# Casting and averaging of the weights moved from ahead of a recurrent scan into its first group

## What is computed

```python
u = x @ W_in + b_in
g = sigmoid(x @ W_gate + b_gate)
h_t = tanh(h_prev @ A + u_t @ Bm)            # 16384 steps, state of 256
y_t = h_t @ C.T + u_t @ D.T
y_t = g_t * y_t + (1.0 - g_t) * x_t
x1 = layernorm(x + (ys @ W_out + b_out + x))
bw = mean(abs(w), axis=1) * sign(w)          # for w1 (4096 x 1024) and w2 (1024 x 4096)
out = layernorm(x1 + gelu(x1 @ bw1.T + b1) @ bw2.T + b2)
```

## Time and profile before

| what | value |
|---|---|
| median of 3 runs | 12,396.43 us (12,390.03 to 12,402.32) |
| the profiled execution: its own time | 12,394.35 us |
| its span on the slowest core, core 4 | 12,392.8 us |
| spans of the eight cores | 12,332.2 to 12,392.8 us |
| PE, matmuls busy | 6,916.0 us (56%) |
| ScalarE busy | 3,273.7 us (26%) |
| VectorE busy | 1,103.9 us (9%) |
| mean granted TensorE clock on core 4 | 0.535 of full speed |
| first tanh of the scan | 734.59 us from the start |

### The profile page before, as it was taken

How to read it: one execution, slowest core, us unless ns; L and a number is a source line. 1 busy time by engine, 2 the same in 40 slices (tenths; PEclk the granted TensorE clock), 3 DMA queues, 4 the chain that set the end, 5 groups by cost and what they waited for, 6 DMA issues and landing times.

```text
span 12392.8 us, 230075 instructions; the slowest of 8 cores (12332.2 to 12392.8 us)
## 1 busy us (share of the span) xinstructions
PE 6916.0 (56%) x92416; PEld 4470.9 (36%) x92416; DVE 1103.9 (9%) x1916; ACT 3273.7 (26%) x17002; POOL 401.8 (3%) x529
## 2 busy tenths in 40 slices
PE   0034445764467545774467544775467645774444
PEld 0023333443335333443335333443335433443323
DVE  0110000210020100210020100200011100210021
ACT  1112222222223222322223222322223222222210
POOL 1000000000000000000000000000000000000000
PEclk9855555555555555555555555555555555555566
DMA  4430001230023101230013201230013200230024
GB/s 120 137 83 1 1 1 31 87 97 1 1 46 121 48 1 26 74 100 17 1 38 110 67 1 21 59 120 17 1 38 98 79 1 14 76 107 6 1 59 131
DMA packets 360872, 631.19 MB, mean 51 GB/s; under 512 B 18272, under 2 KB 191840, under 8 KB 357760
## 3 DMA queue, kind: packets, MB, share of 16 engines
q0 software_dynamic: 110464, 280.89, 8.8%
q1 hardware_dynamic: 249344, 335.58, 8.6%
HBM read 618.23 MB, written 46.14 MB: 54 GB/s over the span
## 4 chain that ended last, share of the span: by engine, by line
PE 45%; DMA 18%; ACT 17%; issue 13%; DVE 5%; ACTq 2%; DVEq 0%; POOLq 0%; POOL 0%; SPq 0%
PE pss L912 18%; ACT h_ring L922 16%; PE psd L192 16%; DMA BW<-bw2d 8%; PE pss L916 4%; PE pss L914 3%; PE pss L915 3%; DMA XSL<-xT 3%; DMA BW<-bw1d 2%; DMA F32P<-w 2%; ACTq L921 1%; DMA bw2d<-RBF 1%; PE pst L192 1%; DMA bw1d<-RBF 1%; ACT H2BF L576 1%
## 5 line engine op out<-in xcount | busy, mean ns | idle before, releaser
L922 ACT ACTIVATE h_ring<-pss 128x2 bf16<-128x2 f32 x16384 | 2921.7, 178 | 8004.1 <-PE pss L916 8003.9
L912 PE MATMUL pss<-h_ring,A_bf 128*128 128x1 bf16 x16383 | 3037.5, 185 | 3355.3 <-ACT h_ring L922 3338.2
L912 PEld LDWEIGHTS pss<-h_ring,A_bf 128*128 128x128 bf16 x16383 | 1764.8, 108 | 5411.2 <-ACT h_ring L922 4954.3
L899 PE MATMUL pss<-ub_ring,I_bf 128*128 128x2 bf16 x16384 | 2965.8, 181 | 1.3 <-DVE ub_ring L463 1.3
L914 PE MATMUL pss<-h_ring,A_bf 128*128 128x1 bf16 x16383 | 2732.3, 167 | 0.0
L915 PE MATMUL pss<-h_ring,A_bf 128*128 128x1 bf16 x16383 | 2711.5, 166 | 0.0
L916 PE MATMUL pss<-h_ring,A_bf 128*128 128x1 bf16 x16383 | 2702.8, 165 | 0.0
L899 PEld LDWEIGHTS pss<-ub_ring,I_bf 128*128 128x128 bf16 x16384 | 1865.8, 114 | 222.1 <-DVE ub_ring L463 1.8
L914 PEld LDWEIGHTS pss<-h_ring,A_bf 128*128 128x128 bf16 x16383 | 1913.2, 117 | 0.0
L915 PEld LDWEIGHTS pss<-h_ring,A_bf 128*128 128x128 bf16 x16383 | 1740.2, 106 | 0.0
L916 PEld LDWEIGHTS pss<-h_ring,A_bf 128*128 128x128 bf16 x16383 | 1710.9, 104 | 0.0
(11 more groups left out here) (91 smaller groups left out, 2148.2 us busy)
## 6 DMA issues: line engine op xcount, KB each, us to landing
BW<-bw2d SPq DMA_DIRECT2D x256, 512.0 KB, 4.4
BW<-bw2d POOLq DMA_DIRECT2D x256, 512.0 KB, 3.9
BW<-bw1d POOLq DMA_DIRECT2D x128, 512.0 KB, 4.8
BW<-bw1d SPq DMA_DIRECT2D x128, 512.0 KB, 4.0
XSL<-xT POOLq DMA_DIRECT2D x32, 1024.0 KB, 11.4
F32P<-w1T SPq DMA_DIRECT2D x8, 2048.0 KB, 9.8
F32P<-w2T SPq DMA_DIRECT2D x32, 512.0 KB, 3.9
F32P<-w SPq DMA_DIRECT2D x32, 512.0 KB, 3.5
```

What stands on the lines that cost most here:

```text
L899: m0 = eng.matmul(p[:, :], I_bf[:], ub_ring[:, :, slot * G + tl: slot * G + tl + 1], start=True, stop=False)
L912: m1 = eng.matmul(p[:, 0:1], A_bf[:, 0, 0:128], rhs0, start=False, stop=False)
L922: sc_.activation(h_ring[:, :, slot * G + tl: slot * G + tl + 1], p[:, :], AFT.Tanh).then_inc(semh["SS"], 1)
```

## The change

The change moves two pieces of the boot into the planning of group 0, behind plan_uub(1). g_wcast now counts on a semaphore of its own, WCQ, and each of its 16 pairs first waits for the scan to have come to step 256 + 24 x pair, at most G - 64. The 40 loads and sums of absolute values (plan_alpha_consts) wait, load by load, for step 28 x k, k = 0 to 39. The scaling of a1n and a2h is a VectorE item of its own behind the sums, and the item of the boot keeps half_col and bgh8 alone, waiting only for the start loads. Each gelu gets one more wait, for that scaling. The load of F32P0 for group 0 waits for WCQ in place of GXQ. The sign passes stay where they were.

```diff
--- before.py
+++ after.py
@@ -110,7 +110,7 @@
            nc.alloc_psum_tensor("pst1", [128, W], F32)]
 
     sem_names = ["LDW", "TS", "SS", "GX", "GXQ", "GHX", "SYQ", "OUT",
-                 "VDS", "SDS", "PEB2", "GB2"]
+                 "VDS", "SDS", "PEB2", "GB2", "WCQ"]
     sem_names += [f"MMS{i}" for i in range(6)]
     semh = {}
     semc = {n: 0 for n in sem_names}
@@ -264,23 +264,24 @@
 
     def g_wcast(g):
         c = 0
+        pj = 0
         for (srcm, dstm) in ((Wg, wg_d), (Wo, wo_d)):
             for k in range(DC):
                 bounce = H2BF[:, 0:D // H, :] if H <= D else H2BF[:, 0:1, 0:D]
+                g.wait_ge(semh["SS"], min(256 + 24 * pj, G - 64))
+                pj += 1
                 if c > 0:
-                    g.wait_ge(semh["GXQ"], c)
+                    g.wait_ge(semh["WCQ"], c)
                 g.dma_start(out=bounce,
                             in_=bass.AP(srcm, k * 128 * D, [[D, 128], [1, D]])
-                            ).then_inc(semh["GXQ"], 16)
+                            ).then_inc(semh["WCQ"], 16)
                 c += 16
-                g.wait_ge(semh["GXQ"], c)
+                g.wait_ge(semh["WCQ"], c)
                 g.dma_start(out=bass.AP(dstm, k * 128,
                                         [[DC * 128, 128], [128 * DC * 128, DC], [1, 128]]),
                             in_=bounce, allow_slow_non_contiguous=True
-                            ).then_inc(semh["GXQ"], 16)
+                            ).then_inc(semh["WCQ"], 16)
                 c += 16
-    em("gpsimd", g_wcast)
-    WCAST_V = bump("GXQ", 16 * 2 * DC * 2)
 
     def f_reg(g):
         g.wait_ge(semh["LDW"], 16 * NLDW)
@@ -292,13 +293,15 @@
     stage_guard = [NONE, NONE]
     sg_guard = [NONE]
 
-    def boot_load(srcm, off, width, buf):
+    def boot_load(srcm, off, width, buf, pace=0):
         guard = stage_guard[buf]
         pre = semc["SYQ"]
 
         def f_load(s, srcm=srcm, off=off, width=width, buf=buf, guard=guard,
-                   pre=pre):
+                   pre=pre, pace=pace):
             st = stageA if buf == 0 else stageB
+            if pace > 0:
+                s.wait_ge(semh["SS"], pace)
             if guard[1] > 0:
                 s.wait_ge(semh[guard[0]], guard[1])
             if pre > 0:
@@ -353,34 +356,42 @@
             (lambda sg: sg[:, 0:D]),
             buf, lv)
 
-    for k in range(FC):
-        buf = k % 2
-        lv = boot_load(w1, k * 128 * D, D, buf)
-        vv = dve_item(
-            [lambda v, kk=k, buf=buf: v.reduce_sum(
-                a1n[:, kk:kk + 1],
-                (stageA if buf == 0 else stageB)[:, 0:D],
-                mybir.AxisListType.X, apply_absolute_value=True)],
-            waits=[("SYQ", lv)])
-        stage_guard[buf] = ("VDS", vv[-1])
-    for k in range(DC):
-        buf = k % 2
-        lv = boot_load(w2, k * 128 * HF, HF, buf)
-        vv = dve_item(
-            [lambda v, kk=k, buf=buf: v.reduce_sum(
-                a2h[:, kk:kk + 1],
-                (stageA if buf == 0 else stageB)[:, 0:HF],
-                mybir.AxisListType.X, apply_absolute_value=True)],
-            waits=[("SYQ", lv)])
-        stage_guard[buf] = ("VDS", vv[-1])
-
-    ALPHA_V = semc["VDS"]
+    def plan_alpha_consts():
+        for k in range(FC):
+            buf = k % 2
+            lv = boot_load(w1, k * 128 * D, D, buf,
+                           pace=min(28 * k, T // 2))
+            vv = dve_item(
+                [lambda v, kk=k, buf=buf: v.reduce_sum(
+                    a1n[:, kk:kk + 1],
+                    (stageA if buf == 0 else stageB)[:, 0:D],
+                    mybir.AxisListType.X, apply_absolute_value=True)],
+                waits=[("SYQ", lv)])
+            stage_guard[buf] = ("VDS", vv[-1])
+        for k in range(DC):
+            buf = k % 2
+            lv = boot_load(w2, k * 128 * HF, HF, buf,
+                           pace=min(28 * (FC + k), T // 2))
+            vv = dve_item(
+                [lambda v, kk=k, buf=buf: v.reduce_sum(
+                    a2h[:, kk:kk + 1],
+                    (stageA if buf == 0 else stageB)[:, 0:HF],
+                    mybir.AxisListType.X, apply_absolute_value=True)],
+                waits=[("SYQ", lv)])
+            stage_guard[buf] = ("VDS", vv[-1])
+
+        alpha_v = semc["VDS"]
+        cva = dve_item(
+            [lambda v: v.tensor_scalar_mul(a1n[:], a1n[:], 1.0 / D),
+             lambda v: v.tensor_scalar_mul(a2h[:], a2h[:], 1.0 / HF)],
+            waits=[("VDS", alpha_v)])
+        return cva[-1]
+
+    cva_v = [0]
     cv = dve_item(
         [lambda v: v.memset(half_col[:], 0.5),
-         lambda v: v.tensor_scalar_mul(bgh8[:], bg8[:], 0.5),
-         lambda v: v.tensor_scalar_mul(a1n[:], a1n[:], 1.0 / D),
-         lambda v: v.tensor_scalar_mul(a2h[:], a2h[:], 1.0 / HF)],
-        waits=[("LDW", 16 * NLDW), ("VDS", ALPHA_V)])
+         lambda v: v.tensor_scalar_mul(bgh8[:], bg8[:], 0.5)],
+        waits=[("LDW", 16 * NLDW)])
     CONSTS_V = cv[-1]
     BOOT_GHX = semc["GHX"]
 
@@ -573,6 +584,7 @@
                     sc_.wait_ge(semh[mg[0]], mg[1])
                     if h2g[1] > 0:
                         sc_.wait_ge(semh[h2g[0]], h2g[1])
+                    sc_.wait_ge(semh["VDS"], cva_v[0])
                     sc_.activation(H2BF[:, f, :], bank_tensor(bi)[:, 0:H],
                                    AFT.Gelu, bias=b1_32[:, f:f + 1],
                                    scale=a1n[:, f:f + 1]).then_inc(semh["SDS"], 1)
@@ -694,7 +706,7 @@
         def f_xq32(sy, s=s, need_out=need_out, syq_pre=syq_pre):
             if s == 0:
                 sy.wait_ge(semh["GHX"], BOOT_GHX)
-                sy.wait_ge(semh["GXQ"], WCAST_V)
+                sy.wait_ge(semh["WCQ"], WCAST_V)
             if need_out > 0:
                 sy.wait_ge(semh["OUT"], need_out)
             if syq_pre > 0:
@@ -957,12 +969,15 @@
     ub_ready[0] = plan_uub(0)
     while pe_weave:
         pe_drain_one()
-
     for g_idx in range(NG):
         if g_idx >= 1:
             ds_io = plan_ds_io(g_idx - 1)
         if g_idx + 1 < NG:
             ub_ready[g_idx + 1] = plan_uub(g_idx + 1)
+        if g_idx == 0:
+            em("gpsimd", g_wcast)
+            WCAST_V = bump("WCQ", 16 * 2 * DC * 2)
+            cva_v[0] = plan_alpha_consts()
         if g_idx >= 1:
             plan_downstream(g_idx - 1, ds_io)
         for tl in range(G):
```

## The result

The changed kernel takes 12,132.24 us (median of 8 runs, 12,122.45 to 12,144.67) against 12,397.3 us before (8 runs in the same measurement, 12,390.03 to 12,406.9): the ratio is 0.9785, 95% interval 0.9774 to 0.9795, 2.15% less time. 12,102 was forecast, so 30 us of the forecast gain are missing.

A forecast was written before the change was run, and what follows sets the result against it. Bound: one serial thread of 16,384 tanh, whatever precedes its first step paid in full. 12,392.8 - 126.2 - 177.2 + 1 + 8 = 12,098.4 us of span, so 12,102 us measured; range 12,070 to 12,140.

The forecast's parts named there:

- the case called the forecast: Whole kernel: front shortened by 295 to 305 us, gelu waits 0 to 20 us, giving 12,090 to 12,120; chance 0.67.
- two rivals: Whole kernel: moved transfers stall group 1's loads, 12,130 (0.10); another slowest core, 12,067 (0.09) or 12,137 (0.08).
- the contention rival: u of group 1: moved transfers lengthen each of 4 XSL loads by 7 us, stalling the scan, +28, 12,130; chance 0.10.
- Part 1: Front, GpSimd's queue: without g_wcast the first sign store comes at 69.5 us in place of 195.72, saving 126.2 us.
- Part 2: Front, VectorE's queue: without the reductions, first XSL load to first tanh takes 69.7 us, not 246.9, saving 177.2 us.
- Part 3: Inside group 0: moved loads and reductions add zero to a scan step and 1 us at u of group 1.
- The load of XSL: Front, slabs of u for group 0: a load takes 10.2 us to its matmul, with 17.4 as the bound.
- Part 4: ScalarE's queue: the added wait before every gelu costs 8 us, full cost 20, none 0, part absorbed by BW1 waits.
- rivals of a loss: Group 0: moved work stretches the scan step, above 0.29 us a step the kernel is slower, 12,421; chance 0.02.
- a sign chain bound by its loads: Front: loads or HBM, not the queued store, bind the sign chain; only 177 us come, 12,228; chance 0.03.
- The spread of the cores: All cores: ends between 12,332 and 12,393 us, fronts alike, so 60 us are made by stalls inside the groups.
- a group that differs by more than 5 us: Scan groups: the prediction is wrong if a group of after differs from one of before by more than some 5 us.

The follow-up runs named there:

- e3: Kernel before with only g_wcast moved into group 0, the sums left in front and no gelu wait added: 12,271.7 us, ratio 0.9900.
- e6: The changed kernel with every pace (wait for a scan step holding back a moved load or cast) taken away: 12,111.7 us, ratio 0.9787.
- e5: The changed kernel with the moved w loads released 160 scan steps later: 12,114.1 us, ratio 0.9781 to before.
- e4: Kernel before with only the loads and sums of absolute values moved, with the gelu waits, g_wcast left in front: 12,251.2 us, ratio 0.9882.
- e7: The changed kernel with sign passes also moved into group 0, on VectorE, and one wait, given twice, before the first gelu only: 11,743.3 us, ratio 0.9481.
- e10: The changed kernel with the added wait ahead of the first gelu only, given there twice, in place of every gelu: 12,091.0 us, ratio 0.9765.
- e11: e10 with one more satisfied wait in ScalarE's queue ahead of the scan: 12,022.0 us, ratio 0.9710 to before.
- e2: Kernel before with one satisfied wait added in front of every gelu and nothing moved: 12,426.9 us, ratio 1.0028.
- e9: Kernel before with one more satisfied wait in ScalarE's queue ahead of the scan: 12,337.2 us, ratio 0.9958.
- e8: The changed kernel with one more satisfied wait in ScalarE's queue ahead of the scan: 12,054.6 us, ratio 0.9733 to before.

## Why the prediction was right, and where its sum was off

The direction, the size and the mechanism of both large parts were right, and 12,132 lies in the range of 12,070 to 12,140. It lies outside the case called the forecast, though, which ended at 12,120, and inside the range because that was drawn wide enough for two rivals. It comes within 2 us of the contention rival's 12,130, but not by that rival's cause. That the range held was in this part luck.

- **Part 1, 126.2 us.** Right: 125.5 (195.72 - 70.20), and e3 alone gives 124.
- **Part 2, 177.2 us.** The mechanism was right, the size 3 us too large (246.9 - 72.8 = 174.1). From XSL to the first tanh it took 436.58 - 363.75 = 72.8 us, not 69.7: the slabs took 17.7, 17.4, 17.2 and 17.2 us and not 17.1 and 16.4, since a load took 11.3 us to its first matmul (363.75 to 375.07) and not 10.2. The sign chain in front, put as unchanged, took 293.6 us (363.75 - 70.20) and not 292.0. With part 1's 0.7 us the front is 5.4 us short of the forecast 303.4.
- **Part 3, 0 for the scan and 1 for u of group 1.** The zero for a scan step is shown right, by e6 at four times the rate of the row that it was taken from. The XSL loads of group 1 were 21.6 us apart (433.17 to 497.86 over three) and not 20.3 as on core 4 of before, 3.7 us over three, of which 1 was in the sum. The contention rival named the place, but its cause is out by e5, and its size was 28. The section Issuing engines are not separate DMA queues of the Trainium skill ("DMA: Bandwidth & Descriptors") says that transfers started by different engines run on the same 16 DMA engines and interleave. That is said of transfers; a scan step makes none, and in e6 the steps beside 209 GB/s were as short as without.
- **The load of XSL, 10.2 us.** That it took 11.3 is not one core's chance. From issue to first matmul, averaged over the eight cores, the third and fourth load of group 0 took 10.3 us in before and 10.4 in e3, but 11.2 in the change, 11.3 in e4 and 11.5 in e5 and e6; in e7 they took 10.6. So the longer load comes with the sums moved, stays with the w loads released later (e5), and is nearly gone with the signs moved as well. The cause is open.
- **Part 4, 8 us.** This is the step that failed in size. The price of a wait, read in the earlier trace rows from one half stage with a wait less, was right: 0.20, 0.67 and 1.64 us against 0.20, 0.66 and 1.63. That part of it is absorbed beside the waits for BW1 was assumed without a row, and the runs speak against it: 25 and 28 us by e10 and e11, and 35 by e2, whose interval of 22 to 46 leaves the 8 out. Whether they cost more than the 20 that were put as full cost can't be told from these intervals.
- **The sum.** 12,102 + 17 to 20 (gelu waits) + 5 (front) + 3 (XSL) = 12,127 to 12,130, against 12,132. The rivals of a loss and of a sign chain bound by its loads are out.
- **The spread of the cores.** The prediction put the 60 us between the cores down to stalls inside the groups. Most of it is another thing, the two step lengths of the last section. The slowest core was one with the longer step in both profiled executions, so this did not enter the difference between them. One of the prediction's signs of being wrong did come, a group that differs by more than 5 us: from core 4 of before to core 6 of the change groups 2, 3 and 6 are 7, 8 and 7 us longer (counted from 0), with the gelu waits in them; the rest of that is open.

What the prediction did not see at all is the late step. It was in the 166 tanh of the earlier trace rows, as part of a mean; it costs before and after alike (257 late steps on core 4 of before, 265 on core 6 of the change), and so did not enter the difference.

## What to carry to other kernels

In front of a serial chain, count what its first step needs, and put the rest of the preparation under the chain: here everything but the start loads and u could go, and 209 GB/s beside the scan cost nothing that could be measured. A satisfied wait is an instruction: on an engine that sits in a tight chain with another it cost 0.05 to 0.06 us at each gelu or pair, so wait once where the queue is in order. And look at the single steps of a chain, not only at their mean: a period in the outliers points to a mechanism.

## What the runs showed of the hardware that was not expected

- One instruction more or less in ScalarE's queue, ahead of a loop with two instructions a step, changes this kernel by 52 to 68 us (e9, e8, e11 against e10), 0.4 to 0.6%, through a delay of 0.28 us at every 64th step.
- Most cores have one of two step lengths, and keep it from the first group to the last. In the same kernel, the same stretch and at the same granted clock of 0.50, core 6 of the change did 663 tanh in 400 us (the rows above), and core 4 did 666:

```profile
1200.00:1600.00 400.00, 118.96 (x666) 0.50 0.01 1
```

Without the late steps a quiet step takes 0.596 to 0.597 us on one kind of core (59 of the 104 cores profiled) and 0.600 on the other (41); four lie between. On core 6 nearly every quiet step takes 0.600 us, on core 4 half of them take 0.593 or 0.594. Over 16,384 steps the 0.003 us are some 49 us. In the profiled executions it was cores 3 and 4 that had the longer step before, cores 0, 1 and 6 after, and others in the experiments, so it does not belong to a core. Each of these executions had at least one core with the longer step, except that of e6, and the slowest core sets the time; e6's, at 12,094.75 us, was the fastest of its five. This is most of the spread of 60 us between the cores in the earlier trace rows: cores 3 and 4 have 12,380.8 and 12,392.8 us, the other six 12,332.2 to 12,357.1. What picks the kind wasn't tried.
